# Tail blocks of a convolution, attention and expert kernel: both halves of the first layer, then both halves of the second, then the turns

## What is computed

```python
gate_logits = xf @ Wg + bg
top_w, top_i = jax.lax.top_k(gate_logits, TOP_K)          # TOP_K = 2
top_w = jax.nn.softmax(top_w, axis=-1)
w_dense = jnp.sum(jax.nn.one_hot(top_i, E) * top_w[..., None], axis=1)
for e in range(E):                                         # E = 8, D = 64, H = 256
    h = jax.nn.gelu(xf @ W1[e] + b1[e], approximate=False)
    out = out + w_dense[:, e:e + 1] * (h @ W2[e] + b2[e])
```

## Time and profile before

| what | value |
|---|---|
| median of 3 runs | 3503.42 us (3501.93 to 3513.58) |
| span of the profiled execution, first to last instruction | 3490.5 us |
| what lies around the span, against the median | 12.9 us |
| first tail transpose on PE | 3096.78 us |
| first and last tail scatter on POOL start | 3118.75 and 3485.30 us |

### The profile page before, as it was taken

One profiled execution on the slowest core, in us unless ns is written; L12 is line 12 of the kernel. 1 busy time (PEld: TensorE's weight loads), 2 busy tenths in 40 slices (PEclk: granted clock), 3 DMA queues, 4 the chain that ended last, 5 costly groups with the idle time before them and its releaser, 6 DMA issues. The chain is left out here.

```text
span 3490.5 us, 60486 instructions
## 1 busy us (share of the span) xinstructions
PE 3003.7 (86%) x16878; PEld 1597.8 (46%) x16878; DVE 2232.8 (64%) x5060; ACT 1883.4 (54%) x3186; POOL 1872.2 (54%) x1837
## 2 busy tenths in 40 slices
PE   3787787989998988989998989899998977589997
PEld 2554555545554454544544444445454443123332
DVE  3677778686958576667768585867676767222222
ACT  2424243365655656565656555565656555357776
POOL 0006144264655647373746465564737374767777
PEclk6878787899999999999999999999999997799999
DMA  8304223142525242343425242424333221234442
GB/s 225 85 22 112 77 80 100 59 113 73 149 69 141 81 127 80 105 109 91 128 69 142 73 136 78 133 80 118 97 92 106 86 78 52 78 103 131 122 104 61
DMA packets 406813, 345.91 MB, mean 99 GB/s; under 512 B 258190, under 2 KB 347029, under 8 KB 400657
## 3 DMA queue, kind: packets, MB, share of 16 engines
q1 hardware_dynamic: 343632, 260.62, 28.4%
q0 software_dynamic: 53760, 78.84, 6.7%
q10 hardware_dynamic: 9088, 2.47, 0.4%
HBM read 261.66 MB, written 147.47 MB: 117 GB/s over the span
## 5 line engine op out<-in xcount | busy, mean ns | idle before, releaser
L640 POOL DMA_INDIRECT rows<-R,place_at x784 | 803.5, 1025 | 570.5 <-issue 513.3
L646 POOL DMA_INDIRECT out<-o_sb,xb x624 | 662.3, 1061 | 703.2 <-DVE o_sb L1479 413.2
L794 ACT ACTIVATE h_sb<-psum,w2b 128x512 f32<-128x512 f32 x624 | 393.6, 683 | 330.5 <-PE psum L978 326.6
L890 PE MATMUL psum<-xpad,conv_w 128*64 128x448 f32 x2688 | 538.3, 552 | 10.0 <-ACT xpad L723 7.5
L978 PE MATMUL psum<-xts,w1b 64*128 64x512 f32 x1248 | 389.1, 699 | 55.8 <-issue 29.3
L987 PE MATMUL psum<-h_sb,w2b 128*64 128x512 f32 x1248 | 352.0, 644 | 47.8 <-ACT h_sb L794 47.2
L890 PEld LDWEIGHTS psum<-xpad,conv_w 128*64 128x64 f32 x2688 | 188.5, 138 | 322.1 <-issue 309.5
L646 POOL DMA_INDIRECT out<-o_sb,xpad x272 | 272.3, 1001 | 107.9 <-issue 92.6
L757 ACT ACTIVATE conv_y<-psum 128x448 f32<-128x448 f32 x112 | 60.4, 540 | 358.2 <-PE psum L890 358.2
L913 PE MATMUL psum<-WT,conv_y 128*112 128x256 f32 x896 | 234.3, 394 | 12.7 <-DVE QT L1402 6.5
L622 POOL TENSOR_TENSOR QT<-QT,q_sum 112x512 f32<-112x512 f32 x112 | 120.4, 1081 | 229.4 <-DVE q_sum L1427 228.0
(11 more groups left out here) (230 smaller groups left out, 5546.0 us busy)
## 6 DMA issues: line engine op xcount, KB each, us to landing
rows<-rows SPq DMA_DIRECT2D x236, 264.0 KB, 6.0
xb<-rows SPq DMA_DIRECT2D x156, 264.0 KB
x_tok<-in_x SPq DMA_DIRECT2D x16, 1568.0 KB, 7.5
w2b<-w2x SPq DMA_DIRECT2D x312, 65.0 KB
w1b<-w1x SPq DMA_DIRECT2D x312, 64.2 KB
xpad<-rows SPq DMA_DIRECT2D x68, 264.0 KB, 2.7
raw<-in_x SPq DMA_DIRECT2D x32, 448.0 KB
raw<-in_x SPq DMA_DIRECT2D x32, 440.0 KB
```

Source lines behind the costliest of these rows:

```text
L640: pool.indirect_dma_start(rows[:, :], bass.IndirectOffsetOnAxis(ap=place_at[:, j:j + 1], axis=0), R[:, j, :], None) \
L646: pool.indirect_dma_start(out_rows, bass.IndirectOffsetOnAxis(ap=block_rows[:, t, COL_ID:COL_ID + 1].bitcast(U32), axis=0), tokens[:, t, : ...
L794: act.activation(h_sb[:, e, q, :], psum[:, HB0 + e, :], ACT.Gelu, bias=w2b[:, i, e, 2 * C + q:2 * C + q + 1]).then_inc(S["h_ready"], 1)
L890: ins = pe.matmul(dst[64 * i:64 * i + 64, 0:BL], conv_w[:, t, :], xpad[:, i, r0:r0 + ROWS, dx:dx + HW], start=(t == 0), stop=(t == 5))
```

## The change

PE's `tail(k)` now runs H0(k), H1(k), Y0(k-1), Y1(k-1), IN(k+2), OUT(k-2). IN is one block further ahead than before, and two INs come before the first H0. ACT's `tail(k)` runs GELU(k, 0), GELU(k, 1), evacuation(k-1), copies(k+2). The number of instructions, their operands, the buffers and the code of DVE, POOL and SP are the same.

```diff
 def tail(k):                       # ACT
     if k == 0:
         tail_x(0)
+        tail_x(1)
     if k < TAIL:
         gelu_tail(k, 0)
-    if k + 1 < TAIL:
-        tail_x(k + 1)
-    if k < TAIL:
         gelu_tail(k, 1)
     if 1 <= k <= TAIL:
         act.wait_ge(S["t_y_half"], 2 * k)
...
+    if k + 2 < TAIL:
+        tail_x(k + 2)
 def tail(k):                       # PE
     if k == 0:
         in_tail(0)
+        in_tail(1)
     if k < TAIL:
         hidden_tail(k, 0)
-    if k + 1 < TAIL:
-        in_tail(k + 1)
+        hidden_tail(k, 1)
     if 1 <= k <= TAIL:
         outputs_tail(k - 1, 0)
-    if k < TAIL:
-        hidden_tail(k, 1)
-    if 1 <= k <= TAIL:
         outputs_tail(k - 1, 1)
+    if k + 2 < TAIL:
+        in_tail(k + 2)
     if 2 <= k <= TAIL + 1:
         out_tail(k - 2)
```

## The result

| what | before | after |
|---|---|---|
| median | 3509.24 us (20 runs) | 3493.34 us (20 runs) |
| ratio of the two, 95% interval | | 0.9966 [0.9952, 0.9981] |
| span of the profiled execution | 3490.5 us | 3491.0 us |
| first tail IN to the end of the span | 393.7 us | 383.0 us |
| of it: first IN to first tail scatter | 21.97 us | 23.19 us |

The kernel became 0.34% faster, 11.9 us of 3500, with an interval of 0.19% to 0.48%. Forecast were 9.5 us, 3493.9 us. That the median of after lies within 0.6 us of that figure is luck: the forecast started from the 3503.42 us of three executions of the kernel before, and its median over 20 is 3509.24. The two medians lie 15.9 us apart, the ratio gives 11.9, the tail of the two traces 10.8.

What follows compares the result with a forecast made beforehand. PE paces the steady tail before, POOL after: 271 scatter steps take 355.7 us instead of 366.55, 10.9 less, minus 1.4 lost at the start, so 9.5 us off 3503.42 gives 3493.9 us; range 3490.5 to 3503.5.

Steps and rivals of the forecast that it cites:

- The bound before: Steady tail: PE nearly full at 5.42 us per block, 0.11 held back by ACT's copies; POOL sets only the end.
- PE like beside like: PE in the tail: adjacent Y pairs, H pairs and eight transposes save 0.10 us each per block, giving 5.01 without the stall.
- POOL as what is late next: Tail scatters: POOL at 5.15 us per block becomes the bound; 271 steps at 1.296 plus pauses make 355.7 us.
- the pauses: POOL in the tail: two pauses of 2 us and two of 0.3, taken as its own program's and unchanged.
- SP and the start: Tail start: loads keep pace at 5.03 us per block; OUT(0) behind IN(4) makes the first scatter 1.4 us later.
- The sum: Whole kernel: last scatter start at 3475.8 instead of 3485.30, 9.5 us earlier, so a median of 3493.9 us.
- The time around the span: Outside the profiled span: the 12.9 us between span and median were taken to stay.
- Rival A: Tail: PE stays the bound at 5.31 us per block if alike pairs save nothing; 4.8 us gained, 3498.6; chance 0.12.
- Rival B: Tail: loads or an unseen loop keep the pace near 5.4 us; nothing moves, 3502 to 3505; chance 0.11.
- Rival C: Tail: PE's waits lower its clock; at 0.87, 23 us more, 3526; chance 0.08, shared with another slower loop.
- The chances: Whole kernel against a 0.3% (10.5 us) border: faster 0.32, within it 0.61, slower 0.07.

Runs made afterwards that it cites:

- the light kernels: Kernel before and changed kernel, each with three instead of four scatters per tail block: first to last scatter 362.1 us (before 366.6) and 337.7 us (16.9 less).
- the kernel at 5.31: Kernel before with IN and copies one block further ahead, nothing put together: period 5.311 us, first to last scatter 361.5 us, first IN to end 393.4.
- the second trace: The changed kernel itself, profiled and timed once more: ratio to before 0.9978 [0.9960, 0.9996], first to last scatter 354.74 us, first IN to end 383.1.

## Why the prediction held

- **The bound before.** Right. The loop through the copies was read as 0.11 us per block, and the kernel with that alone changed has 5.311 instead of 5.416.
- **PE like beside like.** The sum was 5.01 us, 4.81 were measured. All three terms were too small, H the most: I took 0.10 for each by the Y pairs at the end, and H saves 0.20, Y 0.14 and the transposes 0.15 beside the stall. In the trace the saving of H stands at two places: the step to the next product is 0.42 us instead of 0.52 where the shape does not change, and the step after that is again 0.42 instead of 0.53. Why the second is shorter too, no run shows. It cost the forecast nothing: a PE at 5.16 gives the same tail.
- **POOL as what is late next.** Right, by the light kernels: taking a quarter of POOL's work away moves the changed kernel by 16.9 us. The 271 steps were put at 355.7 us and took 354.6. The term that was off is the pauses: 3.9 + 0.6 forecast, 3.6 and nothing measured: the gaps of 0.3 between blocks are not POOL's own, as they are gone with POOL as the bound.
- **SP and the start.** 1.4 us later forecast, 1.2 measured. SP's 5.03 held for its first blocks (5.0 to 5.1 over the tail), and rows are waited for at each IN as said. At the start no further spell at 1.2 GHz came: the one there lasted 6.8 us, as before.
- **The sum.** 9.5 us forecast, 10.8 in the trace (1.2 lost, 12.0 gained), 11.9 by time with 6.6 to 16.8 as the interval. The largest part of the difference between 9.5 and 10.8 is the pauses and delays, 1.1 us. The gain is what was forecast well; the 3493.9 itself was met by luck, as said at the result.
- **The time around the span.** Wrong, though it cost nothing. I took the 12.9 us between the span and the median as fixed. The profiled execution of after took 3493.38 us with a span of 3491.0: 2.4 us lie around it. The rest was the main loop of one quick execution.
- **Rival A**, PE stays the bound, fell with the 4.81 us; its pace was a fair one (361.5 us from first to last scatter for the kernel at 5.31), its start was not, so that kernel gains 0.3 us from the first IN on and not 4.8. **Rival B**, no change from loads, fell: SP kept to 5.0 to 5.1 us per block. **Rival C**, the clock, fell as a bound: PE is busy for 94.5%, and in the profile of after the granted clock is 1.00 from 3116.7 to 3468.3 us. But what it feared does happen, once in the second trace, for 3.4 us and at no cost. By the rule of the Trainium skill named with it (TensorE: Matmul & The Clock Gate, PE-mode transpose) it would hold for much of the tail, and the trace of after does not agree: eight transposes in a row stand in every period at 1.00. In the one spell shown a wait and the transposes stand together, and no run separates them.
- **The chances.** I gave 0.32 to a gain over 0.3% and 0.61 to less. The first timing says 0.34%, the second 0.22% for the same kernel, the trace 10.8 of 3500, 0.31%. It lies on the border, as the text had it. The 0.32 itself does not follow from its terms: a third of 0.64 and the 0.05 are 0.26.

What the prediction did not see is which half of the edit pays. It credited both, and only the look-ahead, with IN and OUT side by side, was needed.

## What to carry to other kernels

When a busy engine is relieved, ask for the sum of what the next one needs, and stop there: bringing PE from 5.42 to 5.16 us per block, beside POOL's 5.15 and its pauses, was worth 12 us, from 5.16 to 4.81 nothing; and in no trace in which PE ran without a wait did its clock fall in the steady tail. Before grouping instructions for the sake of one engine, look for the loop in the timeline that closes through another; without the look-ahead the same grouping cost 81 us. And compare a stretch with the same stretch of another trace, not whole spans, when all else in the kernel is left as it was.

## What the runs showed of the chip

- Float32 products with 512 columns on half the array: two pairs in a row of 64 rows by 128 columns take 1.92 us, two apart 2.12; of 128 rows by 64 columns 1.87 and 2.01. Eight 128x128 transposes in a row take 1.03, two groups of four apart 1.18.
- An indirect scatter of 128 rows costs POOL 1.287 us from start to start when nothing holds it up. Twice in each tail of 272, after the 113th and the 225th, it stands still for 1.3 to 2.2 us more; that both come at the same place of POOL's program in every kernel with 272 scatters is measured, the cause is open and was not tried.
- VectorE's sums with both inputs in SBUF (0.42 us) lengthen a scatter that starts 0.05 to 0.28 us after them, by 0.30 us less that distance, so by up to 0.24 us; in the changed kernel this is 2.1 us in the whole tail.
- The granted clock fell to 1.2 GHz for 3.4 us in the steady tail of two of the four traces with PE's changed order, behind waits of 1.94 and 1.88 us; in the other two, whose longest waits were 2.10 and 1.07 us, it did not.
